# First attention: products for the row maxima on two 64-row halves, rotary halves exchanged by DMA; second attention: gates on GpSimd

## The reference, cut to what matters

```python
# layer 0, H=16 query heads, KV=4 key heads, DH=64
q, k = q*cos + rotate_half(q)*sin, k*cos + rotate_half(k)*sin   # rotate_half: [-t2, t1] of the halves of 64
attn = softmax(einsum(q, k) * DH**-0.5); out = einsum(attn, v) @ Wo
# layer 1, attention over the batch axis, 16 heads of 8
attn = (attn - max(attn)) * 32
gate = gate_a * (gate_b * grep_a - 1.0) + 2.0
attn = softmax(attn + gate * position_bias)
```

## Time and profile before

| what | us |
|---|---|
| median of 3 runs | 1565.05 (1561.4 to 1566.12) |
| profiled execution, its own time | 1566.98 |
| span of its records | 1565.2 |
| PE busy | 1159.0 |
| DVE busy | 1129.2 |
| POOL busy | 835.0 |
| ACT busy | 608.1 |

### The profile page before, as it was taken

The page is one execution under the profiler, slowest core; times in us unless marked ns, Lnnn a source line. Parts: engine busy times, 40 slices in busy tenths (PEclk is TensorE's granted clock), DMA queues, the critical chain, the costliest instruction groups (busy, mean ns, idle before and its releaser), DMA issues. The chain is left out here.

```text
span 1565.2 us, 29826 instructions
## 1 busy us (share of the span) xinstructions
PE 1159.0 (74%) x10864; PEld 749.5 (48%) x10864; DVE 1129.2 (72%) x1571; ACT 608.1 (39%) x1176; POOL 835.0 (53%) x754
## 2 busy tenths in 40 slices
PE   2288999989999899999999446555358776165554
PEld 1135565646656556566666324434126566133343
DVE  2477978768788587787878368984339786568983
ACT  1135545445455364554546123332133330133331
POOL 0267879778788687887878123231035453023320
PEclk9589999999999999999999768987656788668986
DMA  2322113122132121311211000000000000000001
GB/s 65 87 45 59 39 32 66 43 49 51 33 66 43 29 60 32 66 43 37 61 34 31 15 0 1 1 0 0 24 1 1 1 0 1 14 1 0 1 0 54
DMA packets 52197, 46.37 MB, mean 30 GB/s; under 512 B 7734, under 2 KB 50250, under 8 KB 52042
## 3 DMA queue, kind: packets, MB, share of 16 engines
q1 hardware_dynamic: 52042, 44.33, 12.6%
HBM read 6.42 MB, written 2.10 MB: 5 GB/s over the span
## 5 line engine op out<-in xcount | busy, mean ns | idle before, releaser
L664 POOL TENSOR_TENSOR a_p_lo<-a_probs 128x512 f16<-128x512 f32 x384 | 419.8, 1115 | 26.2 <-ACT a_probs L516 22.7
L516 ACT ACTIVATE a_probs<-a_ps_s 128x512 f32<-128x512 f32 x512 | 303.6, 596 | 328.6 <-PE a_ps_s L448 321.1
L600 DVE TENSOR_REDUCE a_nmx<-a_ps_m 128x2 f32<-128x1024 f32 x256 | 311.1, 1216 | 39.3 <-PE a_ps_m L431 37.6
L464 PE MATMUL a_ps_o<-a_v_hi,a_probs 128*128 128x65 f16 x2048 | 238.7, 194 | 7.0 <-POOL a_p_lo L664 7.0
L466 PE MATMUL a_ps_o<-a_v_hi,a_p_lo 128*128 128x65 f16 x2048 | 238.0, 194 | 0.0
L465 PE MATMUL a_ps_o<-a_v_lo,a_probs 128*128 128x64 f16 x2048 | 237.8, 193 | 0.0
L464 PEld LDWEIGHTS a_ps_o<-a_v_hi,a_probs 128*128 128x128 bf16 x2048 | 191.5, 98 | 61.6 <-issue 14.6
L465 PEld LDWEIGHTS a_ps_o<-a_v_lo,a_probs 128*128 128x128 bf16 x2048 | 189.3, 98 | 44.1 <-issue 0.6
L446 PE MATMUL a_ps_s<-a_qq,a_kk 128*128 128x512 f16 x512 | 195.8, 382 | 10.6 <-issue 6.5
L448 PE MATMUL a_ps_s<-a_qq,a_k_l 65*128 65x512 f16 x512 | 196.7, 384 | 0.0
L825 PE MATMUL f_ps_gu<-f_w_gu,f_hqT 128*128 128x352 f32 x256 | 122.9, 643 | 90.5 <-DVE f_h L912 79.5
(11 more groups left out here) (217 smaller groups left out, 2123.5 us busy)
## 6 DMA issues: line engine op xcount, KB each, us to landing
a_qq<-a_rhi SPq DMA_DIRECT2D x128, 128.0 KB, 2.4
a_kk<-a_rhi SPq DMA_DIRECT2D x64, 128.0 KB, 2.4
a_qq<-a_rlo SPq DMA_DIRECT2D x128, 64.0 KB, 2.1
a_k_l<-a_rlo SPq DMA_DIRECT2D x32, 64.0 KB, 2.1
out_x<-x_sb SPq DMA_DIRECT2D x1, 2048.0 KB, 8.7
a_qq<-a_nmT SPq DMA_DIRECT2D x64, 2.0 KB
m_w<-in_wmod SPq DMA_DIRECT2D x2, 384.0 KB
a_probs<-in_wq SPq DMA_DIRECT2D x1, 512.0 KB, 3.5
```

Source lines behind the costliest of these rows:

```text
L464: nc.tensor.matmul(out, hi, v_hi[:, b % 2, kt, g, 0:65], start=(kt == 0), stop=False)
L516: nc.scalar.activation(probs[:, p % 2, kt, h, :], ps_s[:, i % 2, :], ACT.Exp, scale=DH0 ** -0.5).then_inc(exp_done, 1)
L600: nc.vector.tensor_reduce(nmx[:, p % 2, 2 * i:2 * i + 2], ps_m[:, n % 2, :, :], axis=X, op=ALU.max, negate=True).then_inc(free[n % 2], 1)
L664: nc.gpsimd.tensor_tensor(p_lo[:, p % 2, kt, h, :], pr, pr.bitcast(BF16)[:, 1:2 * L:2], ALU.subtract).then_inc(lo_pool, 1)
```

## The change

In the first attention the exchanged weights and the zeroed keys go. A and K make three products instead of six; DVE multiplies the one result by cosine and by sine, and a new item RD (KD for the keys) lets SP issue four DMAs that carry the sine part, 32 rows each, to the exchanged rows of a new tile `rsw`. RS waits for these DMAs. A moves to slot 0, RD stands in slot 1, RS, RH and RL in slots 4, 5 and 6, B in slots 1, 3, 5 and 7, O in slot 2. B's two products are 64 rows deep, one on rows 0 to 63 and one on rows 64 to 127, into different banks. DVE's low parts are tiles 3 and 7. The three DMAs per key head write less (two of 64 KB in place of 128 KB). In the second attention the gates are made by POOL in four operations with drains, behind its product tiles, and DVE's residual of the round before stands behind the scores.

```diff
@@ -145,19 +145,20 @@
             slots[0].append(("W", b))
+        if pair(s + 3):
+            slots[0].append(("A", s + 3))
+            slots[1].append(("RD", s + 3))
+            slots[4].append(("RS", s + 3))
+            slots[5].append(("RH", s + 3))
+            slots[6].append(("RL", s + 3))
             for i in range(4):
-                slots[2 * i].append(("B", s + 2, i))
-        if pair(s + 3):
-            slots[1].append(("A", s + 3))
-            slots[3].append(("RS", s + 3))
-            slots[4].append(("RH", s + 3))
-            slots[5].append(("RL", s + 3))
+                slots[2 * i + 1].append(("B", s + 2, i))
         if pair(s - 2):
-            slots[3].append(("O", s - 2))
+            slots[2].append(("O", s - 2))
@@ -176,11 +177,14 @@
             for m in range(2):
-                slots[2 + 3 * m].append(("K", b, m))
-                slots[4 + 2 * m].append(("KS", b, m))
-                slots[5 + 2 * m].append(("KH", b, m))
-                slots[6 + m].append(("KL", b, m))
+                slots[2 + 2 * m].append(("K", b, m))
+                slots[3 + 2 * m].append(("KD", b, m))
+                slots[5 + 2 * m].append(("KS", b, m))
+            slots[6].append(("KH", b, 0))
+            slots[7].insert(0, ("KL", b, 0))
         if (b := seq(-4)) is not None:
+            slots[0].append(("KH", b, 1))
+            slots[1].append(("KL", b, 1))
...
@@ -241,7 +246,7 @@
-        kk = sb("kk", [128, 2, KV0, 3, L], FP16)
+        kk = sb("kk", [128, 2, KV0, L], FP16)
...
@@ -278,7 +284,7 @@
-        LO_DVE, LO_POOL = (2, 6), (0, 1, 3, 4, 5, 7)
+        LO_DVE, LO_POOL = (3, 7), (0, 1, 2, 4, 5, 6)
@@ -355,7 +361,14 @@
                 kind = it[0]
-                if kind == "RL":
+                if kind in ("RD", "KD"):
+                    key = it[1:]
+                    r = rope[key]
+                    t.jobs(free, job[("A" if kind == "RD" else "K",) + key], 1)
+                    for k in range(4):
+                        src, dst = slice(32 * k, 32 * (k + 1)), slice(32 * (k ^ 1), 32 * (k ^ 1) + 32)
+                        sp.dma_start(rsw[dst, r % 2, :], rcs[src, r % 2, 1, :]).then_inc(rope_swap[r % 2], 16)
+                elif kind == "RL":
@@ -371,9 +384,8 @@
                         rows, g = slice(DH0 * h, DH0 * (h + 1)), 2 * m + h
-                        hi = rhi[rows, r % NR:r % NR + 1, :].to_broadcast([DH0, 2, L])
-                        sp.dma_start(kk[0:DH0, par, g, 0:2, :], hi).then_inc(k_sent[m], 16)
-                        sp.dma_start(kk[DH0:128, par, g, 0:3:2, :], hi).then_inc(k_sent[m], 16)
+                        sp.dma_start(kk[0:DH0, par, g, :], rhi[rows, r % NR, :]).then_inc(k_sent[m], 16)
+                        sp.dma_start(kk[DH0:128, par, g, :], rhi[rows, r % NR, :]).then_inc(k_sent[m], 16)
...
@@ -403,12 +415,10 @@
                     t.seqs(ht_done, b + 1, 1)
-                    for swap in range(2):
-                        out = ps_m[:, n % 2, swap, :]
-                        hi, lo = (w[:, swap, j * 128:(j + 1) * 128] for w in (w_hi, w_lo))
-                        nc.tensor.matmul(out, hi, hT_hi[:, b % 2, :], start=True, stop=False)
-                        nc.tensor.matmul(out, hi, hT_lo[:, b % 2, :], start=False, stop=False)
-                        last = nc.tensor.matmul(out, lo, hT_hi[:, b % 2, :], start=False, stop=True)
+                    hi, lo = (w[:, j * 128:(j + 1) * 128] for w in (w_hi, w_lo))
+                    nc.tensor.matmul(bank, hi, hT_hi[:, b % 2, :], start=True, stop=False)
+                    nc.tensor.matmul(bank, hi, hT_lo[:, b % 2, :], start=False, stop=False)
+                    last = nc.tensor.matmul(bank, lo, hT_hi[:, b % 2, :], start=False, stop=True)
@@ -426,10 +436,10 @@
                                 t.k_rows(b, m)
-                    for k in range(2):
-                        h, qt = divmod(2 * i + k, QT)
-                        last = nc.tensor.matmul(ps_m[:, n % 2, k, :], rhi[:, r % NR, qt * 128:(qt + 1) * 128],
-                                                kk[:, b % 2, 2 * j // G0, 1 + h, :], start=True, stop=True)
+                    for h in range(2):
+                        rows = slice(DH0 * h, DH0 * (h + 1))
+                        last = nc.tensor.matmul(ps_m[:, n % 2, h, :], rhi[rows, r % NR, i * 128:(i + 1) * 128],
+                                                kk[rows, b % 2, 2 * j // G0, :], start=True, stop=True)
...
@@ -544,20 +554,12 @@
             nc.vector.memset(v_hi[:, :, :, :, DH0:DH0 + 1], 1.0).then_inc(ready, 1)
-            nc.vector.memset(kk[DH0:128, :, :, 1, :], 0.0).then_inc(ready, 1)
-            nc.vector.memset(kk[0:DH0, :, :, 2, :], 0.0).then_inc(ready, 1)
             dve.wait_ge(w_hi_done, 3)
-            for whole, hi, lo in ((wq, wq_hi[:, 0, :], wq_lo[:, 0, :]), (wk, wk_hi[:, 0, :], wk_lo[:, 0, :]),
-                                  (wv, wv_hi[:], wv_lo[:])):
-                nc.vector.scalar_tensor_tensor(out=lo, in0=whole, scalar=WSCALE, in1=hi, op0=ALU.mult,
-                                               op1=ALU.subtract)
-            nc.vector.drain()
-            for w, heads in ((wq_hi, H0), (wq_lo, H0), (wk_hi, KV0), (wk_lo, KV0)):
-                w4 = w[:].rearrange("p s (h a c) -> p s h a c", h=heads, a=2)
-                for a in range(2):
-                    last = nc.vector.tensor_copy(w4[:, 1, :, a, :], w4[:, 0, :, 1 - a, :])
-            last.then_inc(swapped, 1)
+            for whole, hi, lo in ((wq, wq_hi[:], wq_lo[:]), (wk, wk_hi[:], wk_lo[:]), (wv, wv_hi[:], wv_lo[:])):
+                last = nc.vector.scalar_tensor_tensor(out=lo, in0=whole, scalar=WSCALE, in1=hi, op0=ALU.mult,
+                                                      op1=ALU.subtract)
+            last.then_inc(split, 1)
@@ -582,7 +584,7 @@
                     t.ropes(rope_sum, r - 1, 1)
-                    nc.vector.tensor_tensor(rcs[:, r % 2, :, :], ps_m[:, n % 2, :, :], cossin[:],
+                    nc.vector.tensor_tensor(rcs[:, r % 2, :, :], ps_m[:, n % 2, 0:1, :].to_broadcast([128, 2, L]), cossin[:],
@@ -597,7 +599,7 @@
                     t.jobs(full, n, 1)
-                    nc.vector.tensor_reduce(nmx[:, p % 2, 2 * i:2 * i + 2], ps_m[:, n % 2, :, :], axis=X, op=ALU.max,
+                    nc.vector.tensor_reduce(nmx[:, p % 2, i:2 * QT:QT], ps_m[:, n % 2, :, :], axis=X, op=ALU.max,
...
@@ -642,9 +644,9 @@
                     r = rope[key]
-                    t.jobs(free, job[("A" if kind == "RS" else "K",) + key], 1)
+                    t.wait(rope_swap[r % 2], (r // 2 + 1) * 64, ROPE16 // 2 * 64)
                     t.ropes(rope_lo, r - 1, 1)
-                    nc.gpsimd.tensor_tensor(rot[:, r % 2, :], rcs[:, r % 2, 0, :], rcs[:, r % 2, 1, :],
+                    nc.gpsimd.tensor_tensor(rot[:, r % 2, :], rcs[:, r % 2, 0, :], rsw[:, r % 2, :],
...
@@ -1380,7 +1385,20 @@
                                             qkvg[:, r % 2, :, D:2 * D], ALU.mult).then_inc(s_mul_pool, 1)
-                pool.wait_ge(gate_ok, r + 1)
+                pool.wait_ge(sig_ok, r + 1)
+                if r >= 1:
+                    pool.wait_ge(gbias_ok, r)
+                nc.gpsimd.tensor_tensor(gate[:], sig[:, r % 2, :, 1, :],
+                                        grep_a[:].unsqueeze(1).to_broadcast([128, B, H1]), ALU.mult)
+                nc.gpsimd.drain()
+                nc.gpsimd.tensor_tensor(gate[:], gate[:], gate_c[:, 0:1, :].to_broadcast([128, B, H1]), ALU.subtract)
+                nc.gpsimd.drain()
+                nc.gpsimd.tensor_tensor(gate[:], gate[:], sig[:, r % 2, :, 0, :], ALU.mult)
+                nc.gpsimd.drain()
+                nc.gpsimd.tensor_tensor(gate[:], gate[:], gate_c[:, 1:2, :].to_broadcast([128, B, H1]), ALU.add)
+                nc.gpsimd.drain()
+                if r >= 1:
+                    pool.wait_ge(score_ok, r)
@@ -1434,16 +1452,6 @@
             for r in range(QT):
-                dve.wait_ge(sig_ok, r + 1)
-                if r >= 1:
-                    dve.wait_ge(gbias_ok, r)
-                nc.vector.tensor_tensor(gate[:], sig[:, r % 2, :, 1, :],
-                                        grep_a[:].unsqueeze(1).to_broadcast([128, B, H1]), ALU.mult)
-                nc.vector.drain()
-                nc.vector.scalar_tensor_tensor(out=gate[:], in0=gate[:], scalar=-1.0, in1=sig[:, r % 2, :, 0, :],
-                                               op0=ALU.add, op1=ALU.mult)
-                nc.vector.drain()
-                nc.vector.tensor_scalar(gate[:], gate[:], 2.0, None, ALU.add).then_inc(gate_ok, 1)
@@ -1456,8 +1464,6 @@
                     score_sum(HB + k, r, 0)
-                if has(r - 1):
-                    residual(r - 1)
@@ -1468,6 +1474,8 @@
                                         ALU.subtract).then_inc(score_ok, 1)
+                if has(r - 1):
+                    residual(r - 1)
@@ -1544,7 +1552,7 @@
     sin = np.sin(emb).T.astype(np.float32) / np.float32(WSCALE)
```

(12 more changed lines are left out.)

21 lines of the change are left out of this document (13 added, 8 removed).

## The result

The changed kernel took **1586.01 us** (median of 4 runs, 1582.8 to 1589.57) against 1565.59 us (1561.4 to 1567.8) for the kernel before on the same chip: ratio 1.0134, 95% interval 1.0103 to 1.0165. It is slower by 20 us. The profiled execution took 1586.86 us with a span of 1585.0, against 1566.98 before.

A forecast was written before the change was run, and what follows sets the result against it. PE was taken to bound the kernel before, and a ring of exchange DMAs through SP's queue the changed one: 1567.0 + 6 (sequences) + 8 (start) - 11 (second attention) = 1570.0 us, range 1520 to 1606.

The forecast's parts named there:

- SP's ring: First attention, ordinary pairs: exchange, sum, rest and their DMA issues close a loop through SP's queue, 10.7 us per pair.
- at 9.2, before the ring comes round: Ordinary pairs: PE's A and DVE's product are ready 9.2 us after RD's issue, so they don't hold the next exchange.
- B saves between 0 and 0.86: Row maxima's 64-row products: PE saves 0 us per pair without overlap of the row halves, 0.86 with it.
- The third rival: PE runs empty at each depth change of B, 1.3 us per pair, no overlap; pair 11.2, total 1593; chance 0.08.
- A sequence: First attention, eight pairs including the steps of W and K: 98.3 us against 97.5, +6 over seven sequences.
- The loop's own turns cost alike before and after: First attention: turning the loop was taken to cost the same in both kernels, so no term was added.
- The start: Up to the first exponential: SP bounds it through K's exchanges and DMAs, 102 us against 93.9, +8.
- The second attention: Gates on POOL, scores no longer waiting for the residual: 4.2 us less in rounds 1 and 2, 11 less together.
- The short ring: Rival: SP's loop takes below 9.6 us, PE and POOL set the pair at 9.6; total 1519; chance 0.27.
- The longer ring: Rival: exchange DMAs land later or issues stall, 11.3 us per turn, 28 us more; total 1598; chance 0.15.
- That PE would still set 10.2: Rival: exchanged halves change nothing in the pair; only the start and second attention count; total 1564; chance 0.02.
- I am wrong if DVE's product releases SP's RD in ordinary pairs: Sign against the forecast: SP's exchange issue in ordinary pairs waiting for DVE's product, not following RL back to back.

The follow-up runs named there:

- Experiments 3: The changed kernel with a fifth 32-row DMA in every exchange, into a tile nobody reads, the rotary sum waiting for it too: 1640.94 us.
- experiment 10: The kernel with the projection one pair earlier and the maxima's DMA first, its exchange moved back behind the rest's DMAs on SP: 1589.98 us.
- experiment 2: The changed kernel with only SP's order altered: the DMAs spreading q, and the key DMAs, go behind the next pair's exchange: 1599.41 us.
- experiment 8: The changed kernel with the projection one pair earlier, the maxima's DMA ahead of the rest's, and the keys' sums spread over two steps: 1526.31 us.
- experiment 1: The changed kernel with 128-row products for the row maxima again, zeroed key copies and larger key DMAs included: 1598.52 us.
- experiment 6: The changed kernel without the exchange, the sine part added to the rows where it lies, so it computes something else: 1494.55 us.

## Why the prediction was right, and where not

The forecast was 1570.0 with a range of 1520 to 1606; the time lies in it, on the slower side that it gave most chance. The point was 16 us low, +3 forecast for +20 measured, and a range of 86 us that holds cases of both signs is easily met. What held is the mechanism. By its steps:

- **SP's ring: right.** Terms forecast and measured: issues and landing 4.07 and 3.99, sum 1.28 and 1.26, low part and rest 2.26 and 2.2, turn without late issues 10.3 and 10.14, ordinary pair 10.7 and 10.73. Late issues were taken as 0.4 per turn; of 509 issues between 280 and 860 us 23 took over 0.85 and cost 19 us together, 0.04 per issue, 0.3 for eight. They come at fixed places of the loop, so a mean over turns hides that some steps always pay for two and others for none. Experiments 3 and 10 show that the ring is on the path.
- **"at 9.2, before the ring comes round": wrong by 1.0.** That chain is a ring of its own and takes 10.24 (experiment 2): the rounding ended at 6.12, but the last score product, behind two more exponentials, started at 7.6, not 6.65. In the changed kernel it hides behind SP's ring, so it did no harm to the number; as a reading it did, because it made SP's order look like the only thing to cut. It takes both cuts (experiments 2, 8 and 10).
- **"B saves between 0 and 0.86": 0.07.** The upper bound came from overlap alone, the lower one from none. The overlap is full (starts 0.003 apart) and is eaten by the changes of depth, (0.313 - 0.220) + (0.319 - 0.215) = 0.197 per product pair, by the medians of experiment 1 at the same places. The third rival had this pause, priced from the modelled tail as eight of 0.16 with no overlap; it is eight of 0.10 beside a full overlap. The Trainium skill says that row groups run concurrently, starts some 4 ns apart (TensorE: Matmul & The Clock Gate, Part 3); the trace agrees, with 3 ns. It also says that changing the tiling mode drains TensorE (TensorEngine Tiling (Array Packing), Key Properties); the trace shows a pause of 0.10 us at each change, as such a drain would make. Weighed singly, as in the prediction, each misled; the two had to be summed.
- **A sequence: mis-sized by 2.7.** It was put at 98.3 and took 101.0 (mean of the four without a loop's turn: 100.9, 100.5, 101.3, 101.2). By steps, the means of these four against the forecast: K's step 16.6 for 16.4, the one behind it 11.5 for 10.7, the next 11.6 for 10.7, W's 17.1 for 16.5, the one behind W's 12.2 for 11.85, the other three 32.0 for 32.1. For the step behind K's the prediction left something out: it put only six of the twelve key DMAs on SP's path, and the other six stand between the next exchange and the maxima. They don't hold the exchange that follows, which goes out 1.0 to 1.9 us after SP's last issue, when DVE's product is there. It is PE that is late: it makes the products of V, it has a part of the step at the lower clock (below), and in three of five sequences it waits 1.1 to 1.3 us for the DMA of the maxima, which the six hold back. No run tells the three apart. The step after that is not the keys' doing. It takes 12.15, 12.13 and 12.12 us for pairs 8, 24 and 40, which stand at the same place of the loop and have two late issues each, and 10.14 for pairs 16, 32 and 48, which have none. W's step took 16.3 three times, and 19.3 once, with an issue of 1.98.
- **"The loop's own turns cost alike before and after": wrong.** By the spacing of the maxima the 16 steps without a turn took 202.25 us for 194.53 before, 7.7 more; those with one took 4.9 and 2.5 more. So a turn of the loop costs 3 to 5 us less than it did. The first six steps after the maxima of pair 2 lost 8.5, which no term has, and the last four 1.5. Together that is the +25.1 for the +6. That 2.7 x 7.25 sequences is 20, close to the miss of 19, is luck: the first steps and the turns offset each other. What makes the first steps so long isn't shown.
- **TensorE's clock: not in the sum.** In the step behind K's, after PE stood idle for 1.4 and 1.75 us, its granted clock (third number from the end) falls to the lower of its two levels, 1.2 GHz, for some 3.4 us:

```profile
574.00:579.00 5.00, 3.88 (x32) 1.82 (x33) 1.99 (x2) 3.36 (x8) 3.94 (x4) 0.66 0.42 96
```

  From 120 to 840 us the time at the lower clock adds up to 14 us in the kernel before, 75 in the changed one, 85 in experiment 2, 38 in experiment 6 and 27 in experiment 8. An ordinary turn of 10.14 us (620.78 to 630.92) has none of it, so it isn't what sets the ordinary pair. The first six steps have 21 us of it, the same steps before 3; it may be part of their 8.5 and of the steps around the keys, but its price wasn't measured apart from the waits that bring it.
- **The start: right**, 101.8 for 102, with the exponential right behind the rounding of pair 2 as forecast. **The tail** and first steps gave 3.5 that were not in the sum.
- **The second attention: 14.4 for 11.** The mechanism was right (the exponential behind its table load, the scores ahead of the residual). From the start of the stretch to the exponential of rounds 0 to 3 the gains are 2.1, 7.9, 12.0 and 14.3; round 1 alone gives 5.8 for 4.2. A gate operation on POOL took 0.46 us, not 0.8, and they end far from the path.
- **The rivals.** The short ring (1519) fell: the exchange's issues had a median of 0.59 us, and a landing of 2.0. The longer ring (11.3) came near only in late turns. That PE would still set 10.2 fell, as PE's own pair is 9.47.
- **"I am wrong if DVE's product releases SP's RD in ordinary pairs".** It did so 19 times in 580 us, while the rest held SP 38 times. Of the 19, six stand behind W, two at the head of K's step where the loop turns, six are the keys' own exchanges, and five are the exchange two steps behind K's (1 to 1.8 us each). The last five are ordinary pairs by the prediction's count, so there the sign came true, for one step in a sequence; in the other ordinary turns the exchange waited for DVE 0.1 us at most. PE's busy share fell to 89.5, not to 80. The 80 came from a PE pair of 8.7; with the 9.47 that it is, a turn of 10.73 gives 88.

Put together: 1570.0 + 19.1 between the marks + 3.5 at the ends - 0.1 at the start - 3.4 in the second attention - 2.3 in the stretches not touched is 1586.8, against 1586.9 of the profiled execution.

The net: the exchange buys PE 0.65 us per pair and more in the steps of K, 53 us in all, and the waiting for it takes 91 back.

## What to carry to other kernels

When work moves from a busy engine to a DMA, look for the rings it closes: through the issuing queue, and through every in-order engine that waits for its result ahead of work that leads back to the next transfer. Add up every one of them before you cut any, as the second longest sets the time once the longest is gone; here the cure was not fewer DMAs but a whole step between issue and use, with the one small DMA that the next pair waits for ahead of the large ones. In one engine's stream, price a row-packed pair together with the change of depth into it and out of it: a lone pair between full-depth products gains next to nothing.

## What the runs showed of the hardware

- Two 64-row products of 512 columns on different row halves start 0.003 us apart and both are over in 0.39 us, where one of full depth takes 0.38 (by the modelled ends). A change from full to half depth costs 0.093 us over the spacing of full-depth products at the same place, the change back 0.104 (changed kernel against experiment 1). A 65-row product beside 128-row ones has no such pause (0.22).
- A DMA of 32 rows of 2 KB takes 0.59 us to issue on SP and lands in 2.0 us, as one of 64 rows of 1 KB does (both 64 KB); 128 KB land in 2.4.
- In the changed kernel 1 issue in 22 takes 0.9 to 2 us in place of 0.6, and mostly at the same places in each turn of the loop; why there isn't shown. In a ring such an issue is paid in full (12.1 for 10.14 with two of them); experiment 8 has as many (30 of 508, 27 us), and its ordinary pairs still take 9.5.
- A low part on POOL (128x512) takes 1.04 us, and 1.48 where one of DVE's overlaps it (medians of experiment 10).
